# Graph network of four layers: the small indirect transfers of the edge lists wait for one another, and three later stages are reordered

## The reference, cut to what matters

```
x = _layernorm(x + _L0_gnn_ref(...))   # normalised neighbour sum of x @ W
x = _layernorm(x + _L1_gnn_ref(...))   # two SAGE layers: h @ W_self + mean @ W_neigh + b
x = _layernorm(x + _L2_gnn_ref(...))   # attention: e = att . leaky(xl[src] + xr[dst]), softmax over dst,
                                       # sum of alpha * xl[src], then @ W_up
x = _layernorm(x + _L3_gnn_ref(...))   # 8 relations: for r: sums = segment_sum(x[src] * (type == r)) / cnt,
                                       # out += mean @ weight[r]; then tanh(u) * z + x * (1 - z), z from w_gate
```

## Time and profile before

| | |
|---|---|
| median of 3 runs | 4061.81 us (4047.09 to 4082.49) |
| the profiled execution | 4085.29 us |
| its span, first to last instruction | 4083.5 us |
| mean granted PE clock | 0.864 |
| busy, share of the span | PE 74%, DVE 46%, POOL 41%, ACT 26% |

### The profile page before, as it was taken

How to read it: one execution, slowest core, us unless ns; L and a number is a source line. 1 busy time by engine, 2 the same in 40 slices (tenths; PEclk the granted TensorE clock), 3 DMA queues, 4 the chain that set the end, 5 groups by cost and what they waited for, 6 DMA issues and landing times. The chain is left out here.

```text
span 4083.5 us, 42432 instructions
## 1 busy us (share of the span) xinstructions
PE 3027.5 (74%) x16465; PEld 1907.4 (47%) x16465; DVE 1897.7 (46%) x3363; ACT 1045.7 (26%) x1358; POOL 1662.9 (41%) x1468
## 2 busy tenths in 40 slices
PE   5999651199316315999799977998977878987966
PEld 5566540088205204997344423435945553333433
DVE  7566640146001302435544442433854354987856
ACT  0133210121000001112221211213834343554433
POOL 3787037400671572000666675761100003776511
PEclk8999975599657657999899988998998989999978
DMA  8666740043101102324555543434467685887442
GB/s 280 150 138 143 297 133 15 26 134 101 32 2 51 49 13 89 115 103 144 162 178 163 178 144 112 143 95 174 171 241 252 213 279 172 295 287 248 147 153 100
DMA packets 305032, 604.50 MB, mean 148 GB/s; under 512 B 95412, under 2 KB 112793, under 8 KB 303452
## 3 DMA queue, kind: packets, MB, share of 16 engines
q1 hardware_dynamic: 109814, 287.24, 20.7%
q0 software_dynamic: 98896, 137.13, 12.8%
q10 hardware_dynamic: 96120, 177.42, 12.3%
HBM read 427.55 MB, written 218.05 MB: 158 GB/s over the span
## 5 line engine op out<-in xcount | busy, mean ns | idle before, releaser
L446 PE MATMUL ps<-wb,xh 128*128 128x256 f16 (+1 forms) x2560 | 451.4, 279 | 205.7 <-issue 165.5
L726 PE MATMUL ps<-sl,x 128*128 128x512 f16 (+1 forms) x1120 | 434.1, 388 | 91.7 <-ACT ue L2236 75.7
L2590 POOL DMA_INDIRECT gm<-YD,gix x195 | 230.4, 1182 | 572.8 <-DMA YD<-yl 479.2
L728 PE MATMUL ps<-sl,x 128*128 128x512 f16 (+1 forms) x1120 | 433.7, 387 | 11.5 <-issue 11.1
L727 PE MATMUL ps<-sl,x 128*128 128x512 f16 (+1 forms) x1120 | 434.1, 388 | 7.9 <-issue 6.6
L446 PE MATMUL ps<-wb,xl 128*128 128x256 f16 (+1 forms) x1280 | 357.6, 279 | 81.2 <-issue 81.2
L446 PEld LDWEIGHTS ps<-wb,xh 128*128 128x128 f16 (+1 forms) x2560 | 258.0, 102 | 255.4 <-issue 182.8
L2567 POOL DMA_INDIRECT gl<-XL,ei x167 | 179.2, 1073 | 427.8 <-DMA XR<-xrn 377.2
L2510 POOL DMA_INDIRECT T<-cnt,adr x167 | 273.7, 1639 | 103.4 <-DMA T<-cnt,adr 43.1
L2541 POOL DMA_INDIRECT rec<-CI,cix x167 | 157.8, 945 | 308.3 <-DMA CI<-hv 254.8
L2393 ACT ACTIVATE ms<-gm,rc 128x1024 f16<-128x1024 f32 x195 | 217.8, 1142 | 152.0 <-DMA gm<-YD,gix 79.9
(11 more groups left out here) (385 smaller groups left out, 6085.9 us busy)
## 6 DMA issues: line engine op xcount, KB each, us to landing
UD<-ue ACTq DMA_DIRECT2D x126, 256.0 KB
yb<-UD SPq DMA_DIRECT2D x126, 256.0 KB, 7.6
YD<-yb ACTq DMA_DIRECT2D x126, 256.0 KB, 3.0
rf<-in_W_early ACTq DMA_DIRECT2D x112, 256.0 KB
sw<-in_W_early SPq DMA_DIRECT2D x112, 256.0 KB
EM<-neg ACTq DMA_DIRECT2D x40, 625.0 KB
eb<-EM SPq DMA_DIRECT2D x9, 2500.0 KB, 9.1
slab<-T SPq DMA_DIRECT2D x27, 625.0 KB, 6.1
```

The costliest lines, as they stand in the source:

```text
L446: i = pe.matmul(ap, l, r, start=(q == 0), stop=(q == len(pairs) - 1))
L726: pe.matmul(ps[0:r, :], high, t[:, 0, :], start=(k == 0), stop=False)
L728: i = pe.matmul(ps[0:r, :], low, t[:, 0, :], start=False, stop=(k == 7))
L2590: pool.indirect_dma_start(out=gm[c % NGB][:, :], out_offset=None, in_=YD, in_offset=bass.IndirectOffsetOnAxis(ap=gix[:, c:c + 1], axis=0), ...
```

## The change

Every transfer of the three lists now waits for the one before it, over one common semaphore `edge_io`, which takes the place of `cg_in`, `ci_in` and `rec_put`. Three later stages change too: 9 units (`AHEAD`) instead of 3 go ahead of the first row block of stage (8); the split of `vv` for the next pass is done inside a pass (tiles 6 and 7) instead of at its end; and in stage (9) the finished tile is written by ACT, right behind its last operation, while SP only loads, as `load_sums` and `load_rest`.

```diff
-AHEAD = 3
+AHEAD = 9
...
-            w.wait_ge(*cg_in("cg"))
+            for s in edge_io:
+                w.wait_ge(*s("cg"))
...
                     for i in range(NT):
...
-                    if 2 * r + j + 2 < 2 * NBR:
-                        low_up(2 * r + j + 2)
+                        if i == 7 and 0 < 2 * r + j < 2 * NBR - 1:
+                            low_up(2 * r + j + 1)
...
-                    if 2 * r + j + 2 < 2 * NBR:
-                        high_up(2 * r + j + 2)
+                        if i == 6 and 0 < 2 * r + j < 2 * NBR - 1:
+                            high_up(2 * r + j + 1)
...
+                if c == LAG2 + 1:
+                    for n in range(AHEAD):
+                        store_unit(n)
...
+                w.wait_ge(*A("on", i))
+                act.dma_start(out[128 * i:128 * i + r, :], t[0:r, :]).then_inc(*out_put[i % 3].tick(i))
...
                 w.wait_ge(*bd_out("bd"))
+                w.wait_ge(*edge_io[0].now())
                 pool.indirect_dma_start(
...
-                    in_offset=bass.IndirectOffsetOnAxis(ap=adr[:, 0, t:t + 1], axis=0)).then_inc(*cg_in.tick("cg"))
+                    in_offset=bass.IndirectOffsetOnAxis(ap=adr[:, 0, t:t + 1], axis=0)).then_inc(*edge_io[0].tick("cg"))
...
             for t in range(ET):
+                w.wait_ge(*edge_io[0].now())
                 pool.indirect_dma_start(
                     out=rec[:, t, 2:3], out_offset=None, in_=CI.rearrange("a b -> (a b)").rearrange("(c d) -> c d", d=1),
...
             for t in range(ET):
+                w.wait_ge(*edge_io[0].now())
                 pool.indirect_dma_start(
                     out=REC, out_offset=bass.IndirectOffsetOnAxis(ap=adr[:, 1, t:t + 1], axis=0), in_=rec[:, t, :],
...
-            w.wait_ge(*rec_put("rec"))
+            for s in edge_io:
+                w.wait_ge(*s("rec"))
...
-            def load_rows(i):
+            def load_sums(i):
...
+            def load_rest(i):
+                r, a = ROWS[i], i % 2
+                s = slice(128 * i, 128 * i + r)
                 if i >= 2:
                     w.wait_ge(*V("o", i - 2))
...
-            load_rows(0)
-            load_rows(1)
-            for i in range(NT):
-                if i + 2 < NT:
-                    load_rows(i + 2)
-                put_out(i)
+            load_sums(0)
+            load_sums(1)
+            load_rest(0)
+            load_rest(1)
+            for i in range(2, NT):
+                load_sums(i)
+                load_rest(i)
```

More of the change, by code:

```diff
@@ L225, in program @@
         slab_w, u_out = [landed(f"slab_w{i}") for i in range(6)], [landed(f"u_out{i}") for i in range(NU)]
-        u_fill, ci_out, ci_in, rec_fill = landed("u_fill"), landed("ci_out"), landed("ci_in"), landed("rec_fill")
-        rec_put, mt_out, rec_in = landed("rec_put"), landed("mt_out"), landed("rec_in")
+        u_fill, ci_out, rec_fill = landed("u_fill"), landed("ci_out"), landed("rec_fill")
+        mt_out, rec_in = landed("mt_out"), landed("rec_in")
         rows_in, em_put = [landed(f"rows_in{i}") for i in range(NG)], landed("em_put")
         dg_in = landed("dg_in")
-        em_in, cg_in = [landed(f"em_in{i}") for i in range(3)], landed("cg_in")
+        em_in, edge_io = [landed(f"em_in{i}") for i in range(3)], [landed("edge_io")]
         wu_in, x2_in, sx_in = landed("wu_in"), landed("x2_in"), [landed(f"sx_in{i}") for i in range(2)]
@@ L2540, in gpsimd @@
             for t in range(ET):
+                w.wait_ge(*edge_io[0].now())
                 pool.indirect_dma_start(
                     out=rec[:, t, 2:3], out_offset=None, in_=CI.rearrange("a b -> (a b)").rearrange("(c d) -> c d", d=1),
-                    in_offset=bass.IndirectOffsetOnAxis(ap=cix[:, t:t + 1], axis=0)).then_inc(*ci_in.tick("ci"))
-            w.wait_ge(*ci_in("ci"))
+                    in_offset=bass.IndirectOffsetOnAxis(ap=cix[:, t:t + 1], axis=0)).then_inc(*edge_io[0].tick("ci"))
+            for s in edge_io:
+                w.wait_ge(*s("ci"))
             w.wait_ge(*V("adr", 1))
@@ L2547, in gpsimd @@
             for t in range(ET):
+                w.wait_ge(*edge_io[0].now())
                 pool.indirect_dma_start(
                     out=REC, out_offset=bass.IndirectOffsetOnAxis(ap=adr[:, 1, t:t + 1], axis=0), in_=rec[:, t, :],
-                    in_offset=None, bounds_check=REC_PAD - 1, oob_is_err=False).then_inc(*rec_put.tick("rec"))
+                    in_offset=None, bounds_check=REC_PAD - 1, oob_is_err=False).then_inc(*edge_io[0].tick("rec"))
             def put_logits(t):
@@ L2944, in load_rows @@
                 sp.dma_start(xr[a][0:r, :], X3[s, :]).then_inc(*zx_in[a].tick(i))
[L2946 to L2949, removed]
             w.wait_ge(*P("lu", ALL_G - 1, NT - 1))
```

## The result

The changed kernel takes 4176.39 us (median of 4 runs, 4160.60 to 4184.84) where the kernel before takes 4054.55 us in the same comparison (4047.09 to 4082.49). The ratio is 1.0283, with a 95% interval of 1.0221 to 1.0345: slower by 122 us. Its profiled execution took 4170.81 us, its span is 4169.0 us, 85.5 us more than that of before, and the mean granted PE clock 0.86.

What follows compares the result with a forecast made beforehand. POOL's chain of 501 waits at X = 3.05 us was taken to start the gathers: 4083.5 + 153 - 43 - 27 - 4 - 16 = 4146.5, 4148 with 1.8 around the span, times 0.994, said as 4125 us; range 3990 to 4270.

Steps and rivals of the forecast that it cites:

- POOL's lists are a chain of their own, and the main stream's gain is not used: Three lists: POOL's 501 waits, not XR, start the gathers, 153 us later, though the main stream wins some 545 us.
- X: Three lists: time from one small transfer's start to the next, 3.05 us, range 2.8 to 3.35.
- rival 2: Three lists: small gathers' round trip may be shorter than a scatter's; X = 2.7, median 3951 us; chance 0.18.
- The gather stage: Gather stage: half of POOL's 63 us of waits for DVE and half of 20 at its end saved, -43 us.
- Stage (7): Ends of passes: half of PE's 55.0 us of waits for DVE saved by the earlier `vv` load, -27 us.
- AHEAD: Row stage: six more units laid over PE's wait of 7.43 us for the first block, -4 us.
- The end stage: End stage: next tile's sums loaded earlier, 2 of 4.7 us saved for each of 8 tiles, -16 us.
- the factor 0.994: Whole kernel: scaling from the profiled execution to the median, 4148 x 0.994 = 4124 us.
- The short trip: Same as rival 2: X = 2.7 in the lists, chain ends at 1922, median 3951 us; chance 0.18.
- The others go on crawling: Beside the lists: even one small transfer at a time disturbs the other engines; about 4700 us; chance 0.05.
- Load makes it dear: Three lists: the main stream's transfers slow each small one, X 3.4 to 4; 4400 us at 3.6; chance 0.13.
- The whole trip takes 2.0 us: Three lists: X = 2.0, chain ends at 1571, median 3600 us; chance 0.03.

Runs made afterwards that it cites:

- experiment 11: The kernel before, unchanged, profiled once more: 4064.23 us, beside 4064.62.
- experiments 1: The kernel before with only the three lists one in flight; AHEAD, stage (7) and end stage as before: 4251.85 us, ratio 1.0379.
- experiment 2: The kernel before with the three later edits alone, no wait in the lists: 4061.25 us, ratio 0.9912.
- 8 and 9: The changed kernel with two and three tiny memsets before each small transfer instead of the wait: 3412.08 and 3496.97 us, ratios 1.0122 and 1.0392.
- experiment 7: The changed kernel with five tiny memsets instead of the wait before each transfer of all three lists: 3703.51 us, ratio 0.912.
- experiment 6: The changed kernel with no waits in the third list, nor in the second from its 61st transfer on: 3799.23 us, ratio 0.9342.

## Why the prediction was right

The predicted time, 4125 us, was 51 us below the measured one, and inside the range. The mechanism was right; that the size came so near owes something to luck, for two errors in X cancel, and so do some of the smaller terms. Point by point:

- **POOL's lists are a chain of their own, and the main stream's gain is not used.** Right, and it is the whole result. The main stream won 632 us (the estimate said 545), the gathers start 174 us later (153), released by the last REC.
- **X.** (2117.93 - 573.36) / 501 = 3.08 us, against 3.05 taken from the scatters of EM; the first transfer starts 4.2 us later than before. Of the 21 us by which the start was missed, 16.5 are X and 4.3 the later first start. The mean came out right, its parts did not. The quiet gather is 2.62 us, and not "about the same as for the scatter" (2.87): the argument of rival 2, that the trip of a 4-byte gather may be shorter than a scatter's, was true by 0.25 us. And load adds not 0.1 to 0.2 but, in the first list, 3.44 - 2.62 = 0.82 us. The two errors cancel, which is luck. The Trainium skill ("DMA: Bandwidth & Descriptors", section "Anatomy of one DMA — SWDGE (gpsimd) path") gives a transfer about 2.0 us fixed. The traces agree roughly for both kinds: behind POOL's own part a quiet scatter takes 1.89 us and a quiet gather 1.68. The X of 2.94 worked out from it was a little over both and 0.5 us too small under load.
- **The gather stage:** -43 said, -51.9 measured. The 63.3 us of POOL's waits for DVE are gone, as was said. But the size is not firm: in the second profile of the kernel before (experiment 11) the same stage takes 795.4 us and not 823.1, against which the gain is 24.
- **Stage (7):** -27 said, -16.7 measured. The size lies inside its bounds (0 to -55), but the waits that it was priced by are not the ones that gave it. The waits of 11 to 15 us for `yb` went, but others took most of their place: 55.0 us before, 48.6 after, now for the split of `vv` (waits in 3090:3540):

```profile
DVE vv L1711 <- ACT vv L1968: 49.1, 12, 16.3
PE ps L446 <- DVE vv L1711: 48.6, 8, 15.5
```

What the stage also lost is a wait that the prediction did not name, one of 21.3 us of PE's transposes in the kernel before:

```profile
3061.66 1.11 PE L451 MATMUL ps<-ident,z 128*128 128x128 f32 x4 [21.28 <-DVE yb L1743]
```

It is there in experiments 1 and 11 too (21.3 and 21.4 us), and it is gone in experiment 2 and in the changed kernel. DVE's `yb` stood behind its split of `vv`, which had waited 23.5 us for ACT's half.

- **AHEAD:** -4 said; the row stage is 1.2 us shorter, too little to tell.
- **The end stage:** -16 said, -17.3 measured. In the chain that ended last a tile takes 18.05 and 18.45 us (`ro` starts at 4013.95, 4032.00 and 4050.45) instead of 20.0, and the transfer of `ro` 6.7 to 6.9 us instead of 5.2. That fits loads that now share the DMA engines, as was said; no run tested it.
- **From the sum to the median.** The terms came to +63 us on the span and measured +85.5, an error of 22 us. The later start of the gathers accounts for 21; the gather stage (9 too little) and stage (7) (10 too much) cancel. The larger part of the 51 us, 29, is the factor 0.994: the profiled execution of before lay 31 us above its median, that of after 6 us below. A factor from one execution among three runs was worth less than it was given; without it the forecast would have been 4148.
- **The rivals.** The short trip (X = 2.7) was right of the quiet gather (2.62) and wrong of the sum; it fell with the load and with the scatters. "The others go on crawling" fell with the first window above. "Load makes it dear" held for the first list alone, where X reached its lower end, 3.44. "The whole trip takes 2.0 us" fell: the quickest list ran at 2.90.
- **A step that the prediction took for granted** did not hold: that the crawl belongs to the kernel. In two of the comparisons the kernel before takes 3370 us, most likely because nothing crawls. The changed kernel was not run beside them. An estimate: its chain of waits does not depend on the crawl, so its gathers would start near 2118 and it would take some 2118 + 2018 = 4136 us against 3370.

The time goes by the start of the gathers above all. Over all 14 profiles that start moves from 1396 to 2118 us, and what follows it (span less the first start of `gl`) stays between 2011 and 2140: 2139.5 and 2123.4 in the two profiles of the kernel before, 2111.7 in experiment 2, 2051.1 after, 2018.0 and 2015.1 in 8 and 9.

## What to carry to other kernels

A wait for the landing of each small indirect transfer turns a list of them into a serial chain of about 2.6 to 3.4 us a transfer, so before such waits are put in, multiply by the length of the list and see what stands behind it in the same program: here 501 of them were longer than all the slack of their engine. If the aim is to spare other engines, pace the transfers only as far as those need it and only while they have work: five tiny instructions between two transfers did it for 2.11 us each in the mean (ratio 0.912), two in flight left part of the crawl and came as far (0.903), one in flight cost 3.08 (1.028). And compare against the kernel before in every comparison: it took 4055 to 4088 us in four comparisons and 3370 in two, most likely because the pattern that was the whole reason for the edit, PE at 0.15 of its time, was absent there.

## What the runs showed of the hardware

**The crawl looks like a lack of instructions, but not of their delivery.** The DMA part of the page counts, by queue, the packets of a stretch; q8 and q14 carry instructions. In the kernel before, in 569:781:

```profile
q8 instruction: 1, 0.02, 0.0%
```

In the 254 us after it q8 brings 16 packets, and PE with its weight loads runs 2051 + 2052 instructions: 256 for a packet. In the crawl it is 1 packet and 127 + 127 instructions; beside the first list of experiment 7 it is 23 packets and 2872 + 2873. Over the whole changed kernel it is 129 packets and 2 x 16465 instructions, 255 for a packet. So q8 brings PE's instructions in blocks of about 256, and the question is whether the crawl waits for a block. It does not. The packet of this list starts at 583.13 and takes 0.93 us, the next one starts at 814.85. The windows between it and the next, and behind that:

```profile
583.13:814.85 231.72, 30.45 (x124) 20.36 (x123) 16.12 (x34) 14.15 (x35) 147.28 (x156) 0.51 0.07 18
814.85:830.10 15.25, 15.12 (x136) 12.79 (x134) 8.85 (x12) 7.83 (x12) 0.00 (x0) 0.99 0.01 2
```

247 instructions in 232 us, spread over all of the crawl, and then a block of 270 in 15 us. In experiment 6 one block comes at 1766.7 and the next at 1857.2, with the whole crawl of 1773 to 1832 between them. If the crawl were a wait for blocks, PE would run through each one at its usual pace and then stand. The packets are few because PE is slow, and not the other way round.

PE's timeline with two in flight, once the crawl has set in (640 to 670), has its gaps released by nothing, and its starts lie at multiples of about 0.70 us from one another:

```profile
651.08 0.37 PE L446 MATMUL ps<-wb,xh 128*98 128x256 f16 x1 [1.54 <-issue]
651.80 0.43 PE L446 MATMUL ps<-wb,xh 128*98 128x256 f16 x1 [0.35 <-issue]
653.20 0.37 PE L446 MATMUL ps<-wb,xl 128*98 128x256 f16 x1 [0.97 <-issue]
654.61 0.66 PE L446 MATMUL ps<-wb,xh 128*98 128x256 f16 x2 [1.03 <-issue]
```

Each matmul itself is as long as at the same clock just before (0.42 us at 647); it is the next one that does not come. What holds it back between the delivered block and the engine stays open.

**The granted clock follows the crawl and does not make it.** It is 0.52 in the crawling lists, the lower of its two levels (1.2 GHz), and 0.97 beside the first list of experiment 7, next to the upper one (2.4 GHz). In the timeline of experiment 6 the order can be read: the gaps start at 1771.4, while matmuls still take 0.38 us, and only from 1778.22 on do they take 0.59.

**Pace and crawl.** Beside the first list, where the machine crawls: at one small transfer per 1.27 us (no cap, or three in flight) PE does 0.13 to 0.15 of its time; at 1.99 (memsets) and 3.44 (one in flight) 0.94. With two in flight it does 0.26 at one per 1.4 us and 0.67 and 0.93 in the stretches at one per 1.6 and 1.9. Where it does not crawl: 0.93 at 1.54. The crawl outlasts its cause: behind the last start of the second and the third list (1245.8 and 1565.7) PE's single matmuls go on until 1269 and 1584, some 20 us.
